# Layer 1 of the second half with W1 as weights, in a DLRM tower kernel

## The chip, the cores and the metric

The kernel runs on one core of one Trainium2 chip. The metric is the device time of one execution in microseconds (us).

## What is computed

Every one of 512 samples has 26 embedding rows of 128 numbers, looked up in 26 tables by `ids`, and one row of dense features. The dot products of all pairs of these 27 vectors and the dense row go through a tower of three layers:

```python
combined = concat([dense[:, None, :], e], axis=1)             # 512 x 27 x 128
pairs = einsum('bfd,bgd->bfg', combined, combined)[:, iu, ju]  # 351 pairs, i < j
h = concat([dense, pairs, dense], axis=1)                      # 512 x 607
h = maximum(h @ W_top1 + b_top1, 0.0)                          # 512 x 512
h = maximum(h @ W_top2 + b_top2, 0.0)                          # 512 x 256
y = h @ W_top3                                                 # 512 x 1
```

## The kernel before

All of it is written out by hand for five engines, with semaphores, and each engine runs its own list in order. Ten small tables are looked up as products with one-hot matrices (L415, L416, the first 50 us); the rows of the other sixteen tables are gathered by 64 indirect DMAs that GpSimd issues (L369), four to a group of 32 samples, and turned on TensorE by `turn_group` (L426) and, for the last group, in two halves by `turn_last` (L434). ScalarE copies each turned group into `eT`, where every sample has its vectors side by side.

`gram_chunk(n)` (L450) makes the dot products of 32 samples from `eT`: eight products in full float32, for which the trace shows 16 weight loads and 16 matmuls. Chunk 15 is made in two halves, the second one once the second half of the last group (group 16) is in `eT`. The two halves of `gram` hold chunks of even and odd number, and ScalarE and VectorE each copy half the rows of a chunk to `dots` (L680, L703). Four chunks are one tile of 128 samples. For each tile VectorE turns and repacks `dots` into `band` (`flip_tile`, L967 to L972; `flip_last_tile`, L988 to L996, where ScalarE takes a part), and TensorE turns `band` in three pieces so that the pairs lie on the partitions (`turn_pairs`, L459; `turn_last_pairs`, L467 and L472). ScalarE rounds the result to `pT_hi` (a type, float32r, whose products take one pass), and VectorE keeps the rest in `pT_lo`. In the same way all weights and activations are a high and a low part, and a product of two such operands is three matmuls: high by high, high by low, low by high.

**Layer 1 has two forms.** For the first half of the samples (tiles 0 and 1) W1 is the weight operand and the 256 samples of the half are the moving one, so its output has the units of layer 1 on the partitions, as layer 2 needs it. For tiles 2 and 3 it is the other way round (`rows_products`, L552): the 128 samples of a tile are the weights and 512 or 256 columns of W1 move past them. The output has samples on the partitions, so it is rectified into `h1_rows` (L834, L1013), turned by `turn_h1` (L595), rounded to `h1_hi` by `h1_rows_split` (ScalarE, L703) and the rest put in `h1_lo` by `h1_rows_rest` (VectorE, L1020). In tile 3 this goes in two banks, numbered 3 (units 256 to 511) and 4 (units 0 to 255).

Layer 2 of a tile starts with the bias, `layer2_bias` (L524, L525): two products of a single partition, a row of ones by the high and the low part of b2. Then come four steps of three products (`layer2_step`, L529 to L531). Layer 3 is one operation of VectorE for a tile (L1041).

PSUM tiles are used in turn: `look` has two banks in the order of `LOOK_ORDER`, and `look_bank` waits until the bank's use two places earlier has been read. `turn_pairs(2)` is two places behind layer 2 of tile 0, so it waits for `layer3(0)` on VectorE. `late` has two banks in the order of `LATE_ORDER`.

Of the kernel before, what the change touches and what calls it, by code (L numbers as in the profile page):

```python
# [24 lines left out]
P = 128  # L25
# [112 lines left out]
LOOK_ORDER += [("group", 14), ("group", 15), ("h1", 2), ("group", 16), ("turn", 3), ("layer2", 2), ("h1", 3), ("h1", 4)]  # L138
# [18 lines left out]
def late_on_act(what):  # L157
    return what[0] == "table" or what in (("rows", 2), ("rows", 4))
# [6 lines left out]
ROWS_OUT = 3 * 32 + NF  # L165


def build(nc, dense, ids_rows_first, ids_rows, ids_bcast, gathered, padded, w1, w2, b2, w3, out):
    with ExitStack() as ctx:
# [35 lines left out]
        b2_sb = sb("b2_sb", [1, H2])  # L205
        b2_hi = sb("b2_hi", [1, H2], F32R)
        b2_lo = sb("b2_lo", [1, H2], F32R)
        one_row = sb("one_row", [1, P], F32R)
# [3 lines left out]
        h1_rows = x_rows[:, :, :].rearrange("p t d -> p (t d)")  # L212
# [38 lines left out]
        w_sum = sem("w_sum")  # L251
        w_hi = sem("w_hi")
# [10 lines left out]
        pT_lo_ready = sem("pT_lo_ready")  # L263
        y_ready = sem("y_ready")
# [38 lines left out]
        def _(sp):  # L303
# [37 lines left out]
            sp.dma_start(b2_sb[:, :], b2).then_inc(w_in, 16)  # L341
            sp.dma_start(w3_sb[:, :], w3.to_broadcast([P, H2])).then_inc(w_in, 16)
            wait_look_done(sp, ("layer2", TILES - 2))
            sp.wait_ge(y_ready, 2)
# [30 lines left out]

        def late_layer2(t):

            q = 0 if t == TILES - 1 else CHUNK_Q // 2
            return gram[:, t // 2, q:q + H2 // P, :].rearrange("b q n -> b (q n)")

        @block.tensor
        def _(pe):
# [130 lines left out]
            def layer2_bank(t):  # L513
                if t in (0, 2):
                    return look[:, LOOK["layer2", t] % 2, 0:H2]
                return late_layer2(t)

            def layer2_bias(t):
                if t in (0, 2):
# [49 lines left out]
            def rows_3(n):  # L569
                return late[:, LATE["rows", n] % 2, 0:H1 // 2], slice(H1 // 2, H1) if n == 3 else slice(0, H1 // 2)  # L570
# [570 lines left out]
```

## Time and profile before

| what | us |
|---|---|
| median of 3 runs (112.5 to 112.81) | 112.67 |
| the profiled execution | 112.72 |
| its span, first to last instruction | 111.0 |
| TensorE busy in the span | 103.1 |
| VectorE, ScalarE, GpSimd busy | 79.7, 74.0, 71.9 |

The granted TensorE clock is 1.00 of full speed over the span. The 1.72 us between the profiled execution's time and its span lie before its first and after its last instruction. Names such as `late` and `look` in the rows are the PSUM tiles; the type "f32" of a matmul stands for float32 and for float32r. In the trace a matmul's length includes the time in which it drains, so lengths of neighbours overlap; the time that one takes from TensorE is read from start to start, or from the chain. In the chain, "x12" is twelve instructions of one line in a row.

### The profile page before, as it was taken

How to read it: one execution, taken by the hardware profiler on the slowest of the kernel's cores; microseconds unless marked ns; L12 is line 12 of the kernel's file. 1: busy time of each engine (PE TensorE's matmuls, PEld its weight loads, DVE VectorE, ACT ScalarE, POOL GpSimd, SP SyncE). 2: the span in 40 equal slices, each digit the busy share in tenths (PEclk: the TensorE clock that was granted, in tenths of full speed). 3: DMA queues.
4: the chain of work that ended last, by engine and by line, in shares of the span. 5: the costliest groups of instructions: out<-in, count | busy, mean ns of one | idle time of the engine just before them, and what ended most of it. 6: DMA issues, size and time to landing. Idle time of an engine off the chain costs nothing.

```text
span 111.0 us, 1932 instructions
## 1 busy us (share of the span) xinstructions
PE 103.1 (93%) x670; PEld 90.3 (81%) x670; DVE 79.7 (72%) x184; ACT 74.0 (67%) x131; POOL 71.9 (65%) x73
## 2 busy tenths in 40 slices
PE   3999999699999999989999989999999999999971
PEld 3965788577888888667999979999999998988760
DVE  5389999959999998972177996988348750596421
ACT  3347988999999999698578754759342563744030
POOL 6977778778877777777777777777777772000000
DMA  1899876892598279994211122112221111000000
GB/s 42 247 285 348 260 248 180 321 301 66 159 289 310 64 294 269 368 350 125 56 47 47 47 62 59 50 47 53 56 62 47 47 47 47 6 0 3 0 0 1
DMA packets 7195, 14.74 MB, mean 133 GB/s; under 512 B 1937, under 2 KB 2578, under 8 KB 7186
## 3 DMA queue, kind: packets, MB, share of 16 engines
q1 hardware_dynamic: 4850, 10.36, 27.9%
q0 software_dynamic: 2048, 4.20, 14.0%
q8 instruction: 5, 0.08, 0.4%
q10 hardware_dynamic: 288, 0.07, 0.3%
q14 instruction: 4, 0.03, 0.1%
HBM read 14.62 MB, written 0.00 MB: 132 GB/s over the span
## 4 chain that ended last, share of the span: by engine, by line
PE 50%; ACT 20%; DMA 13%; DVE 10%; issue 3%; SPq 1%; ACTq 0%; DVEq 0%
PE gram L450 25%; DMA table<-in_tbl 13%; ACT eT L703 7%; ACT table_hi L703 6%; DVE onehot L909 5%; PE late L552 5%; PE late L501 4%; DVE table_lo L903 3%; ACT distance L719 3%; PE look L426 3%; ACT onehot L723 2%; PE gram L529 1%; PE late L415 1%; PE look L529 1%; PE late L416 1%
## 5 line engine op out<-in xcount | busy, mean ns | idle before, releaser
L369 POOL DMA_INDIRECT e_rows<-in_gathered,idx x64 | 68.4, 1068 | 19.4 <-issue 19.4
L415 PE MATMUL late<-onehot,table_hi 128*128 128x512 f32 x84 | 34.3, 409 | 2.2 <-ACT eT L703 1.4
L416 PE MATMUL late<-onehot,table_lo 128*128 128x512 f32 x84 | 33.2, 395 | 0.0
L450 PE MATMUL gram<-eT 128*123 128x108 f32 x256 | 29.6, 271 | 0.6 <-ACT dots L703 0.3
L909 DVE TENSOR_SCALAR onehot<-ids,row_of_partition 128x512 fp32r<-128x512 int32 x69 | 29.8, 480 | 0.3 <-DMA ids<-in_ids_bcast 0.3
L450 PEld LDWEIGHTS gram<-eT 128*123 128x123 f32 x256 | 28.6, 187 | 1.0 <-ACT eT L703 0.5
L415 PEld LDWEIGHTS late<-onehot,table_hi 128*128 128x128 f32 x84 | 16.0, 190 | 8.0 <-ACT eT L703 2.3
L680 DVE COPY dots<-gram 32x216 f32<-32x216 f32 (+3 forms) x34 | 12.6, 371 | 11.2 <-PE gram L450 10.7
L703 ACT ACTIVATE dots<-gram 32x216 f32<-32x216 f32 (+1 forms) x34 | 11.2, 330 | 11.9 <-PE gram L450 11.7
L416 PEld LDWEIGHTS late<-onehot,table_lo 128*128 128x128 f32 x84 | 16.1, 191 | 3.0
L903 DVE TENSOR_TENSOR table_lo<-table,table_hi 128x384 fp32r<-128x384 f32 (+2 forms) x29 | 15.5, 536 | 2.7 <-ACT table_hi L703 2.7
L703 ACT ACTIVATE table_hi<-table 128x1024 fp32r<-128x1024 f32 (+2 forms) x11 | 11.1, 1013 | 5.3 <-DMA table<-in_tbl 5.3
L703 ACT ACTIVATE eT<-look 128x512 f32<-128x512 f32 (+1 forms) x18 | 11.6, 649 | 2.4 <-PE look L426 2.2
L703 ACT ACTIVATE eT<-late 128x512 f32<-128x512 f32 x10 | 11.0, 1097 | 0.4 <-PE late L416 0.4
L719 ACT ACTIVATE distance<-ids,row_of_partition 128x512 f32<-128x512 int32 x15 | 10.6, 706 | 0.0
L723 ACT ACTIVATE onehot<-distance 128x512 fp32r<-128x512 f32 x15 | 9.5, 633 | 1.3
L426 PE MATMUL look<-ident,e_rows 128*128 128x128 f32 x60 | 8.8, 272 | 0.0
L426 PEld LDWEIGHTS look<-ident,e_rows 128*128 128x128 f32 x60 | 7.1, 142 | 0.8
L618 PE MATMUL gram<-ident 128*128 128x128 f32 x18 | 4.2, 430 | 1.7 <-POOL ident L356 1.7
L618 PEld LDWEIGHTS gram<-ident 128*128 128x128 f32 x18 | 3.9, 331 | 1.7 <-POOL ident L356 1.7
L703 ACT ACTIVATE pT_hi<-look 126x384 fp32r<-126x384 f32 (+1 forms) x4 | 3.0, 754 | 1.6 <-PE look L467 1.5
L834 ACT ACTIVATE x_rows<-late 128x512 f32<-128x512 f32 (+1 forms) x2 | 1.0, 490 | 4.5 <-PE late L552 4.5
(103 smaller groups left out, 112.9 us busy)
## 6 DMA issues: line engine op xcount, KB each, us to landing
table<-in_tbl SPq DMA_DIRECT2D x7, 512.0 KB, 3.6
ids<-in_ids_bcast SPq DMA_DIRECT2D x10, 256.0 KB, 4.0
w_raw<-in_w SPq DMA_DIRECT2D x7, 256.0 KB
table<-in_tbl SPq DMA_DIRECT2D x2, 640.0 KB, 3.8
e_rows<-in_gathered,idx POOLq DMA_INDIRECT x64, 2.8
table<-in_tbl SPq DMA_DIRECT2D x2, 256.0 KB, 4.1
x_rows<-in_dense SPq DMA_DIRECT2D x1, 256.0 KB, 4.7
w_sb<-in_w SPq DMA_DIRECT2D x1, 128.0 KB
```

The costliest lines, as they stand in the source:

```text
L369: pool.indirect_dma_start(out=e_rows[:, c % GROUPS_AHEAD, k, :], out_offset=None, in_=gathered[:, :], in_offset=bass.IndirectOffsetOnAxis( ...
L415: pe.matmul(bank, table_hi[0:KP, i % 2, c, :], hot, start=c == 0, stop=False)
L416: last = pe.matmul(bank, table_lo[0:KP, i % 2, c, :], hot, start=False, stop=c == CHUNKS[i] - 1)
L426: last = pe.transpose(bank[:, k * P:(k + 1) * P], e_rows[:, c % GROUPS_AHEAD, k, :], ident[:, :])
L450: last = pe.matmul(gram[0:ROWS_OUT, n % 2, q, 0:QUADS * NG_COL], eT_flat[:, b * SLOTS:b * SLOTS + ROWS_OUT], eT[:, b:b + QUADS, 0:NG_COL], ...
L618: pe.matmul(gram[:, 0, 0, :], ident[:, :], ident[:, :], start=True, stop=True)
L680: return copy(dots[rows, t % 2, :, q0 + a:q0 + b], gram[rows, n % 2, a:b, j * NG_COL:(j + 1) * NG_COL].rearrange("f q g -> f g q"))
L703: return act.activation(dst, src, ACT.Copy)
L719: act.activation(distance[0:KP, n % 2, :], ids[0:KP, i % IDS_RING, :], ACT.Abs, bias=row0[CHUNKS[i]][0:KP, c:c + 1], scale=-1.0).then_inc( ...
L723: act.activation(onehot[0:KP, (free + OH_RING) % OH_RING, :], distance[0:KP, n % 2, :], ACT.Relu, bias=1.0, scale=-1.0).then_inc(onehot_ac ...
L903: dve.tensor_tensor(table_lo[0:KP, i % 2, a:c, :], table[0:KP, i % 2, a:c, :], table_hi[0:KP, i % 2, a:c, :].bitcast(F32), ALU.subtract).t ...
L909: dve.tensor_scalar(onehot[0:KP, n % OH_RING, :], ids[0:KP, i % IDS_RING, :], row0[CHUNKS[i]][0:KP, c:c + 1], None, ALU.is_equal).then_inc ...
```

## The change

- Layer 1 of tiles 2 and 3 is made one block of 128 units at a time, with W1 as weights and the tile's 128 samples as the moving operand. `rows_products` becomes `tile_products`: 12 products of 512 columns in tile 2 become 48 of 128 columns, and 24 products of 256 columns in tile 3 (6 for the dense row, 18 for the pairs) become 12 and 36 of 128 columns.
- The output has the units on the partitions. `turn_h1` and its eight transposes, the rectifying copies to `h1_rows` and three uses of `look` go. `h1_tile_split` (ScalarE) rectifies and rounds straight from `late`, and `h1_tile_rest` (VectorE) makes the low part.
- `layer2_bias` is one product of all 128 partitions: `bias_rows` has ones in rows 0 and 32 and zeros elsewhere, `b2_rows` the high part of b2 in row 0 and the low part in row 32. VectorE fills both with four memsets before it waits for the weights, and b2 is loaded to 33 partitions instead of one.
- Layer 2 of tile 2 goes to the bank of group 16. Its steps 2 and 3 move from before the last layer 1 to behind it. The last tile's layer 2 takes the products with `h1_hi` first and those with `h1_lo` behind them.
- On VectorE the low part of tile 2 moves from between the two halves of chunk 15's copies to before chunk 14's; `layer3(2)` moves behind the low parts of tile 3. `layer3(2)` reports on `y_ready`, and the output's DMA waits for that alone.

```diff
-LOOK_ORDER += [("group", 14), ("group", 15), ("h1", 2), ("group", 16), ("turn", 3), ("layer2", 2), ("h1", 3), ("h1", 4)]
+LOOK_ORDER += [("group", 14), ("group", 15), ("group", 16), ("turn", 3)]
...
-        one_row = sb("one_row", [1, P], F32R)
+        b2_sb = sb("b2_sb", [LO_ROW + 1, H2])
+        b2_rows = sb("b2_rows", [P, H2], F32R)
+        bias_rows = sb("bias_rows", [P, P], F32R)
...
+        def tile_units(n):
+
+            return late[:, LATE["rows", n] % 2, 0:(4 if n == 2 else 2) * P].rearrange("u (k b) -> u k b", b=P)
+
+        def tile_h1(h1, n):
+
+            ks = {2: slice(0, N1), 3: slice(2, N1), 4: slice(0, 2)}[n]
+            t = min(n, TILES - 1)
+            return h1[:, ks, t % 2 * P:(t % 2 + 1) * P]
...
+            if t == 2:
+                return look[:, LOOK["group", NCK] % 2, 0:H2]
             q = 0 if t == TILES - 1 else CHUNK_Q // 2
             return gram[:, t // 2, q:q + H2 // P, :].rearrange("b q n -> b (q n)")
...
             def layer2_bias(t):
-                if t in (0, 2):
+                if t == 0:
                     look_bank(("layer2", t))
+                elif t == 2:
+                    wait_look_done(pe, ("group", NCK))
                 else:
                     pe.wait_ge(dots_act, NCK if t == 3 else NCK - 1)
                     pe.wait_ge(dots_dve, NCK if t == 3 else NCK - 1)
-                pe.matmul(layer2_bank(t), one_row[0:1, :], b2_hi[0:1, :], start=True, stop=False)
-                pe.matmul(layer2_bank(t), one_row[0:1, :], b2_lo[0:1, :], start=False, stop=False)
+                pe.matmul(layer2_bank(t), bias_rows[:, :], b2_rows[:, :], start=True, stop=False)
...
-            def rows_products(t, bank, weights, units, start=False, stop=False):
+            def tile_products(t, out, weights, unit, start=False):
...
+                units = slice(unit * P, (unit + 1) * P)
                 for side, w, k in weights:
                     if k == KT:
-                        left = (x_hi, x_lo)[side][:, cols]
-                        right = w[:, KT, units]
+                        last = pe.matmul(out, w[:, KT, units], (x_hi, x_lo)[side][:, cols], start=start, stop=False,
+                                         skip_group_check=True)
                     else:
-                        left = (pT_hi, pT_lo)[side][0:KR, k, pair_cols]
-                        right = w[0:KR, k, units]
-                    last = pe.matmul(bank, left, right, start=start, stop=stop)
+                        last = pe.matmul(out, w[0:KR, k, units], (pT_hi, pT_lo)[side][0:KR, k, pair_cols],
+                                         start=start, stop=False, skip_group_check=True)
                     start = False
                 return last
...
             def layer1_rows_2():
-                bank = late_bank(("rows", 2))
-                units = slice(0, H1)
-                rows_products(2, bank, DENSE, units, start=True)
+                late_bank(("rows", 2))
+                out = tile_units(2)
+                for n in range(N1):
+                    tile_products(2, out[:, n, :], DENSE, n, start=n == 0)
...
-                for k in range(KT):
-                    rows_products(2, bank, [(0, w1_hi, k), (0, w1_lo, k)], units)
+                for n in range(N1):
+                    tile_products(2, out[:, n, :], [(0, w, k) for k in range(KT) for w in (w1_hi, w1_lo)], n)
                 wait_look_done(pe, ("turn", 2))
-                rows_products(2, bank, [(1, w1_hi, k) for k in range(KT - 1)], units)
-                rows_products(2, bank, [(1, w1_hi, KT - 1)], units, stop=True).then_inc(late_full, 1)
...
+                for n in range(N1):
+                    last = tile_products(2, out[:, n, :], [(1, w1_hi, k) for k in range(KT)], n)
+                last.then_inc(late_full, 1)
+
+            LAST_UNITS = [(3, 0, 2), (3, 1, 3), (4, 0, 0), (4, 1, 1)]
 
             def layer1_rows_3_dense():
-                for n in (3, 4):
-                    late_bank(("rows", n))
-                    bank, units = rows_3(n)
-                    rows_products(3, bank, DENSE, units, start=True)
+                for bank, j, n in LAST_UNITS:
+                    if j == 0:
+                        late_bank(("rows", bank))
+                    tile_products(3, tile_units(bank)[:, j, :], DENSE, n, start=j == 0)
...
             def layer1_rows_3():
                 for k in range(KT):
                     pe.wait_ge(pT_hi_ready, 3 + k + 1)
-                    for n in (3, 4):
-                        bank, units = rows_3(n)
-                        rows_products(3, bank, [(0, w1_hi, k), (0, w1_lo, k)], units)
+                    for bank, j, n in LAST_UNITS:
+                        tile_products(3, tile_units(bank)[:, j, :], [(0, w1_hi, k), (0, w1_lo, k)], n)
                 wait_look_done(pe, ("turn", 3))
                 pe.wait_ge(pT_lo_ready, KT - 1)
-                for n in (3, 4):
-                    bank, units = rows_3(n)
-                    rows_products(3, bank, [(1, w1_hi, k) for k in range(KT - 1)], units)
-                    rows_products(3, bank, [(1, w1_hi, KT - 1)], units, stop=True).then_inc(late_full, 1)
-
-            def turn_h1(n, ks):
-                bank = look_bank(("h1", n))
-                wait_late_done(pe, ("rows", n))
-                for k in ks:
-                    last = pe.transpose(bank[:, k * P:(k + 1) * P], h1_rows[:, k * P:(k + 1) * P], ident[:, :])
-                last.then_inc(look_full, 1)
+                for bank, j, n in LAST_UNITS:
+                    last = tile_products(3, tile_units(bank)[:, j, :], [(1, w1_hi, k) for k in range(KT)], n)
+                    if j:
+                        last.then_inc(late_full, 1)
 
...
             def layer2_rows_3():
-                wait_look_done(pe, ("h1", 3))
-                for k in (2, 3):
-                    layer2_step(3, k, False)
-                wait_look_done(pe, ("h1", 4))
-                for k in (0, 1):
-                    last = layer2_step(3, k, k == 1)
+                t = TILES - 1
+                rows = slice(t % 2 * P, (t % 2 + 1) * P)
+                for n, ks in ((3, (2, 3)), (4, (0, 1))):
+                    pe.wait_ge(h1_hi_ready, n + 1)
+                    for k in ks:
+                        pe.matmul(layer2_bank(t), h1_hi[:, k, rows], w2_hi[:, k, :], start=False, stop=False)
+                        pe.matmul(layer2_bank(t), h1_hi[:, k, rows], w2_lo[:, k, :], start=False, stop=False)
+                    wait_late_done(pe, ("rows", n))
+                    for k in ks:
+                        last = pe.matmul(layer2_bank(t), h1_lo[:, k, rows], w2_hi[:, k, :], start=False,
+                                         stop=n == 4 and k == ks[-1])
                 last.then_inc(last_full, 1)
...
             layer1_rows_2()
             turn_last(0)
             gram_chunk(14)
-            turn_h1(2, range(N1))
             turn_last(1)
             gram_chunk(15, range(CHUNK_Q // 2))
             gram_chunk(15, range(CHUNK_Q // 2, CHUNK_Q))
             layer1_rows_3_dense()
             layer2_first_half(1)
-            layer2_rows_2((0, 1))
+            layer2_rows_2((0,))
             turn_last_pairs(0)
-            layer2_rows_2((2,))
+            layer2_rows_2((1,))
             turn_last_pairs(1)
             turn_last_pairs(2)
-            layer2_rows_2((3,))
             layer2_bias(3)
             layer1_rows_3()
-            turn_h1(3, (2, 3))
-            turn_h1(4, (0, 1))
+            layer2_rows_2((2, 3))
             layer2_rows_3()
...
+            def h1_tile_split(n):
+                if n == 2:
                     wait_look_full(act, ("layer2", 0))
                 else:
                     act.wait_ge(last_full, 1)
-                wait_look_full(act, ("h1", n))
-                copy(h1_hi[:, ks, t % 2 * P:(t % 2 + 1) * P],
-                     look[:, LOOK["h1", n] % 2, :].rearrange("n (k b) -> n k b", k=N1)[:, ks, :]).then_inc(h1_hi_ready, 1)
+                wait_late_full(act, ("rows", n))
+                act.activation(tile_h1(h1_hi, n), tile_units(n), ACT.Relu).then_inc(h1_hi_ready, 1)
...
-            copy(one_row[:, :], one_col[0:1, :])
-            copy(b2_hi[:, :], b2_sb[:, :]).then_inc(w_hi, 1)
+            act.wait_ge(bias_zero, 4)
+            copy(b2_rows[0:LO_ROW + 1, :], b2_sb[:, :]).then_inc(w_hi, 1)
...
-            relu_rows(2, slice(0, H1))
+            h1_tile_split(2)
             last_group(0)
             dots_chunk(14)
             last_group(1)
-            h1_rows_split(2, slice(0, N1))
             last_dots()
             flat_half()
             first_band_block()
             turn_hi(3)
-            relu_rows(4, slice(0, H1 // 2))
-            h1_rows_split(3, slice(2, N1))
-            h1_rows_split(4, slice(0, 2))
+            h1_tile_split(3)
+            h1_tile_split(4)
...
+            dve.memset(b2_rows[:, :].bitcast(F32), 0.0).then_inc(bias_zero, 1)
+            dve.memset(bias_rows[:, :].bitcast(F32), 0.0).then_inc(bias_zero, 1)
+            dve.wait_ge(bias_zero, 2)
+            dve.memset(bias_rows[0:1, :].bitcast(F32), 1.0).then_inc(bias_zero, 1)
+            dve.memset(bias_rows[LO_ROW:LO_ROW + 1, :].bitcast(F32), 1.0).then_inc(bias_zero, 1)
...
+            def h1_tile_rest(n):
                 dve.wait_ge(h1_hi_ready, n + 1)
-                dve.tensor_tensor(h1_lo[:, ks, cols],
-                                  look[:, LOOK["h1", n] % 2, :].rearrange("n (k b) -> n k b", k=N1)[:, ks, :],
-                                  h1_hi[:, ks, cols].bitcast(F32), ALU.subtract).then_inc(look_dve, 1)
+                dve.scalar_tensor_tensor(out=tile_h1(h1_lo, n), in0=tile_units(n), scalar=0.0,
+                                         in1=tile_h1(h1_hi, n).bitcast(F32),
+                                         op0=ALU.max, op1=ALU.subtract).then_inc(late_dve, 1)
...
+            h1_tile_rest(2)
             dots_chunk(14)
             last_dots(0)
-            h1_rows_rest(2, slice(0, N1))
             last_dots(1)
             flip_last_tile()
             layer3(1)
             turn_lo(3)
+            h1_tile_rest(3)
+            h1_tile_rest(4)
             layer3(2)
-            relu_rows_3()
-            h1_rows_rest(3, slice(2, N1))
-            h1_rows_rest(4, slice(0, 2))
             layer3(3)
```

## Rows read from the trace of the kernel before

**Rows 1.** The page, part 1: busy time by engine.

```profile
PE 103.1 (93%) x670; PEld 90.3 (81%) x670; DVE 79.7 (72%) x184; ACT 74.0 (67%) x131; POOL 71.9 (65%) x73
```

**Rows 2.** Windows: busy time and count of each engine in two stretches of the end.

```profile
core 0: us, PE busy (x) PEld busy (x) DVE busy (x) ACT busy (x) POOL busy (x), PEclk, DMA share, GB/s
98.00:103.00 5.00, 5.00 (x35) 4.33 (x36) 3.81 (x13) 1.85 (x5) 0.00 (x0) 1.00 0.00 2
103.00:106.90 3.90, 2.89 (x23) 2.38 (x22) 1.39 (x6) 1.07 (x3) 0.00 (x0) 1.00 0.00 0
```

**Rows 3.** Chain that ended last, 90 to 98 us: start, length, what.

```profile
90.19 2.79 PE late L552 x12
...
93.20 1.71 PE gram L450 x16
94.91 0.44 PE look L595 x4
...
97.27 0.72 PE late L552 x6
```

**Rows 4.** The same chain where layer 2 of tile 2 begins.

```profile
100.03 0.31 PE look L524
100.34 0.12 PE look L525
100.46 0.31 PE look L529
100.77 0.12 PE look L530
```

**Rows 5.** The same chain from the last layer 1 to the end.

```profile
102.84 1.99 PE late L552 x15
...
104.93 0.44 DVE x_rows L1013
...
105.50 0.42 PE look L595 x2
...
106.90 0.38 PE gram L529
...
108.47 0.13 PE gram L531
```

**Rows 6.** Timeline of TensorE and its weight loads: start, length, engine, line, instruction.

```profile
97.01 0.19 PEld L552 LDWEIGHTS late<-w_hi,x_hi 128*128 128x128 f32 x1
97.12 0.19 PEld L552 LDWEIGHTS late<-table_lo,x_hi 128*128 128x128 f32 x1
...
97.04 0.36 PE L552 MATMUL late<-w_hi,x_hi 128*128 128x256 f32 x1
97.24 0.28 PE L552 MATMUL late<-table_lo,x_hi 128*128 128x256 f32 x1
```

**Rows 7.** Timeline of VectorE and the weight loads, 84 to 88 us.

```profile
84.49 1.08 DVE L967 STREAM_TRANSPOSE flip<-dots 128x864 f32<-128x864 f32 x1
...
87.25 0.14 DVE L1041 DVE_READ_ACCUMULATOR look<-look,w_sb 128x1 f32 x1
...
87.45 0.36 PEld L459 LDWEIGHTS look<-ident,band 128*126 128x126 f32 x3
```

**Rows 8.** Timeline of TensorE and ScalarE around gram chunk 14's end.

```profile
94.74 0.60 PE L595 MATMUL look<-ident,x_rows 128*128 128x128 f32 x4
95.18 0.38 PE L434 MATMUL look<-ident,e_rows 128*128 128x128 f32 x2
...
94.94 0.69 ACT L703 ACTIVATE dots<-gram 32x216 f32<-32x216 f32 x2 [1.03 <-PE gram L450]
95.66 0.40 ACT L703 ACTIVATE eT<-look 128x256 f32<-128x256 f32 x1
```

**Rows 9.** Timeline of VectorE and ScalarE, the last tile's pairs.

```profile
100.14 0.40 DVE L996 COPY band<-flat 128x238 f32<-128x238 f32 x1
...
99.71 0.32 ACT L703 ACTIVATE band<-flat 128x126 f32<-128x126 f32 x1
```

More of the change, by code:

```diff
@@ L157, in late_on_act @@
 def late_on_act(what):
-    return what[0] == "table" or what in (("rows", 2), ("rows", 4))
+    return what[0] == "table"
 LATE_ACT = [w for w in LATE_ORDER if late_on_act(w)]
@@ L165 @@
 ROWS_OUT = 3 * 32 + NF
+LO_ROW = 32
 def build(nc, dense, ids_rows_first, ids_rows, ids_bcast, gathered, padded, w1, w2, b2, w3, out):
@@ L251, in build @@
         w_sum = sem("w_sum")
+        bias_zero = sem("bias_zero")
         w_hi = sem("w_hi")
@@ L263, in build @@
         pT_lo_ready = sem("pT_lo_ready")
+        third_full = sem("third_full")
         y_ready = sem("y_ready")
@@ L600, in layer2_rows_2 @@
                     layer2_bias(2)
-                    wait_look_done(pe, ("h1", 2))
+                    wait_late_done(pe, ("rows", 2))
                 for k in ks:
@@ L604, in layer2_rows_2 @@
                 if ks[-1] == N1 - 1:
-                    last.then_inc(look_full, 1)
+                    last.then_inc(third_full, 1)
             def layer2_rows_3():
-                wait_look_done(pe, ("h1", 3))
-                for k in (2, 3):
-                    layer2_step(3, k, False)
-                wait_look_done(pe, ("h1", 4))
-                for k in (0, 1):
-                    last = layer2_step(3, k, k == 1)
+                t = TILES - 1
[9 more added lines that the diff above has]
+                                         stop=n == 4 and k == ks[-1])
                 last.then_inc(last_full, 1)
@@ L828, in h1_split @@
                         "n (k b) -> n k b", k=2), ACT.Relu).then_inc(h1_hi_ready, 1)
-            def relu_rows(n, units):
-                if n > 2:
-                    wait_look_full(act, ("h1", 2))
-                wait_late_full(act, ("rows", n))
-                act.activation(h1_rows[:, units], late[:, LATE["rows", n] % 2, 0:units.stop - units.start],
-                               ACT.Relu).then_inc(late_act, 1)
-            def h1_rows_split(n, ks):
-                t = min(n, TILES - 1)
-                if t == 2:
+            def h1_tile_split(n):
+                if n == 2:
                     wait_look_full(act, ("layer2", 0))
@@ L1008, in turn_lo @@
                                           ).then_inc(pT_lo_ready if k else look_dve, 1)
-            def relu_rows_3():
-                wait_look_full(dve, ("h1", 2))
-                wait_late_full(dve, ("rows", 3))
-                dve.tensor_scalar(h1_rows[:, H1 // 2:], late[:, LATE["rows", 3] % 2, 0:H1 // 2], 0.0, None, ALU.max
-                                  ).then_inc(late_dve, 1)
-            def h1_rows_rest(n, ks):
-                t = min(n, TILES - 1)
-                cols = slice(t % 2 * P, (t % 2 + 1) * P)
+            def h1_tile_rest(n):
                 dve.wait_ge(h1_hi_ready, n + 1)
-                dve.tensor_tensor(h1_lo[:, ks, cols],
-                                  look[:, LOOK["h1", n] % 2, :].rearrange("n (k b) -> n k b", k=N1)[:, ks, :],
-                                  h1_hi[:, ks, cols].bitcast(F32), ALU.subtract).then_inc(look_dve, 1)
+                dve.scalar_tensor_tensor(out=tile_h1(h1_lo, n), in0=tile_units(n), scalar=0.0,
+                                         in1=tile_h1(h1_hi, n).bitcast(F32),
+                                         op0=ALU.max, op1=ALU.subtract).then_inc(late_dve, 1)
             def h1_rest(h):
@@ L1034, in layer3 @@
             def layer3(t):
-                if t in (0, 2):
+                if t == 0:
                     wait_look_full(dve, ("layer2", t))
@@ L1038, in layer3 @@
                 else:
-                    dve.wait_ge(last_full, 1 + t // 2)
+                    if t == 2:
+                        dve.wait_ge(third_full, 1)
+                    else:
+                        dve.wait_ge(last_full, 1 + t // 2)
                     bank = late_layer2(t)
@@ L1042, in layer3 @@
                                                 op0=ALU.max, op1=ALU.mult, accum_out=y[:, t:t + 1])
-                done.then_inc(look_dve if t in (0, 2) else y_ready, 1)
+                done.then_inc(y_ready if t else look_dve, 1)
             dots_chunk(0)
@@ L1067, in _ @@
             dve.wait_ge(w_hi, K1 + N1 + 1)
-            dve.tensor_tensor(b2_lo[:, :], b2_sb[:, :], b2_hi[:, :].bitcast(F32), ALU.subtract).then_inc(w_lo, 1)
+            lo_row = slice(LO_ROW, LO_ROW + 1)
+            dve.tensor_tensor(b2_rows[lo_row, :], b2_sb[lo_row, :], b2_rows[lo_row, :].bitcast(F32), ALU.subtract
+                              ).then_inc(w_lo, 1)
             h1_rest(0)
```

13 lines of the change are left out of this document (3 added, 10 removed).

## Prediction

> **What bounds the kernel now.** I read the page's busy times first, then the windows of the end, then the chain, then the timelines where the chain changes engine. TensorE is busy 103.1 of 111.0 us, far ahead of VectorE with 79.7 [rows 1]. In the windows the reader should see two regimes. From 98 to 103 us TensorE has no free time. From 103 to 106.9 it is busy 2.89 of 3.90 us, because layer 1's last output waits to be turned and rounded [rows 2]. So TensorE work taken away or added before about 105 us counts in full unless a wait stands behind it. After that, latency between engines counts.
>
> **Pitches.** A matmul with weights of its own takes from start to start: 2.79/12 = 0.2325 us with 512 moving columns; 0.72/6 = 0.12 with 256, or closer, from 107.28 to 108.47 in ten steps behind the first product of the last layer 2, 0.118; 1.71/16 = 0.107 for the gram's 123 weight and 108 moving columns; 0.44/4 = 0.110 for a transpose of 128 by 128 [rows 3, 5]. From 256 to 512 columns the pitch doubles, from 256 to about 110 it hardly falls. A float32r weight load shows the floor: two follow each other by 0.11 us (97.01, 97.12), and the matmul that starts with its load is 0.36 us long where the next is 0.28 [rows 6]. The changed layer 1 has 128 moving float32r columns, which no row shows. The bounds are 0.059 us (half of 0.118, if only moving columns counted) and 0.2325 (the 512-column price, if short float32r products ran at a quarter of the rate). I take 0.109, between the gram and the transposes, which are nearest in both shapes.
>
> **Tile 2's layer 1.** 48 x 0.109 = 5.23 for 2.79 [rows 3]: +2.44. It stands between two blocks of a full TensorE.
>
> **The turn of tile 2.** Its four transposes, 0.44, go [rows 3], but they cover a wait. Without them `turn_last(1)` starts at 94.74 instead of 95.18, the first half of chunk 15 at 94.96, and the second half wants its weights after eight more instructions (0.86) less the 0.11 by which a load runs ahead, at 95.7. That half needs group 16 in `eT`. ScalarE copies chunk 14's dots from 94.94 and then group 16 from 95.66 for 0.40, so until 96.06 [rows 8], and neither moves relative to chunk 14. The stall is 0.36 plus about 0.04 for the release. The transposes' 0.44 becomes a wait of 0.40: -0.04.
>
> **Tile 3's layer 1.** Dense part: 12 x 0.109 = 1.31 for 0.72 [rows 3], +0.59. Pairs: 36 x 0.109 = 3.92 for 18 x 0.118 = 2.12, +1.80.
>
> **The bias.** The chain spends 0.31 on the first one-partition product, 0.12 on the second and 0.31 on the first full product behind them; the next full one takes 0.12 [rows 4]. So a step from full height to one partition or back costs 0.19 beyond the pitch. One product of full height leaves 0.12 + 0.12 of 0.74: -0.50 per tile, four tiles. For tiles 1, 2 and 3 TensorE is full and all of it counts: -1.50. For tile 0, at about 84 us, it does not. Behind its layer 2 and a gram chunk comes `turn_pairs(2)`, which waits until `layer3(0)` has read the bank. VectorE begins to repack tile 2's pairs at 84.49, driven by chunk 11 and not by layer 2, and ends `layer3(0)` at 87.39; the weight load of `turn_pairs(2)` starts at 87.45 [rows 7]. With 0.50 less work TensorE arrives at 86.95 and waits 0.50: nothing gained. If the cover were absent, this would be worth -0.50.
>
> **The end.** Now 15 of layer 1's 18 products are done at 104.83, so the last at 104.83 + 3 x 0.118 = 105.18, and the last product of layer 2 at 108.60 [rows 5]. Of these 3.42 us twelve products take 1.42. The other 2.00 are latency: rectifying (VectorE, 0.44), four transposes, rounding and low part, one behind the other.
> After the change bank 3 is complete six products (0.65) before the end E of layer 1. ScalarE's rectifying and rounding is one operation of 256 columns, 0.40 [rows 8], the low part on VectorE another, 0.44 [rows 5]. With 0.2 for draining and release, the high part of bank 3 is there at E, its low part at E+0.45, those of bank 4 at E+0.6 and E+1.05. TensorE runs layer 2 of tile 2, steps 2 and 3, until E+0.71 and asks for these four at E+0.71, E+1.18, E+1.4 and E+1.9. None is late. So -2.0, and the two moved steps cost the same 0.71 in their new place.
> Do the moved steps leave a hole where they stood? They covered the last tile's pairs. Let T be the end of chunk 15 (97.1 now). `band` is ready on ScalarE at 100.03 (T+2.9) and on VectorE at 100.54 (T+3.4) [rows 9]. With the low part of tile 2 out of VectorE's way they can only come earlier, and TensorE has the dense part, 1.31, layer 2 of tile 1, 13 x 0.118 = 1.53, and bias and a step, 0.47: and asks for them at T+3.3 and T+3.8: no wait either way. The rounding of the first piece (0.3 for the transpose, 0.4 on ScalarE) lands within 0.05 of when it is wanted.
>
> **At nothing.** The four memsets stand where VectorE next waits for the weight loads, before the first gram chunk's copies. b2's load to 33 partitions is queued on SyncE ahead of w3's to 128, and both are waited for together, as before. ScalarE and VectorE each handle one narrow operation as before. If this cover were gone it would be a few tenths. The output DMA waits for one semaphore instead of two; `layer3(2)`, now behind the low parts, ends over 0.5 us before `layer3(3)` can begin. VectorE's early low part of tile 2 waits for ScalarE's; queued behind it are only chunk 14's dots, a gram chunk (1.71) later.
>
> **Sum.** 2.44 - 0.04 + 0.59 + 1.80 - 1.50 - 2.0 = +1.3 us. The profiled execution took 112.72, its span 111.0 and 1.72 around it, which I leave alone. It is 0.05 above the median of 112.67. So 114.0.
>
> **Rivals.**
> *A, the forecast* (0.57): weight loads set the pitch, 0.107 to 0.111. With the smaller or larger of them the sum moves by 0.2.
> *B, the two hidden waits are not there* (0.11). If ScalarE's copy of group 16 and `layer3(0)` are not what TensorE meets, 0.40 and 0.50 come back: 113.1. Against it stand the times of [rows 7, 8]; for it, that a wait inferred to within 0.1 us can shrink.
> *C, faster: short products are cheap* (0.10). If a float32r load can hide beneath a matmul faster than 0.11, all 96 products gain. The point at which the change breaks even is 0.109 - 1.3/96 = 0.095 us. At 0.059 the 96 products take 4.8 less: 109.2, or some tenths more since the pairs' repacking would then be waited for. For it: no row has a stream of float32r loads bound by nothing else. Against it: the loads of [rows 6], and a gram that gains nothing from having only 108 columns.
> The Trainium skill (TensorE: Matmul & The Clock Gate, Back-to-back issue gap) puts a sustained stream of load and matmul pairs at about 81 ns for 128 columns. By that figure the sum would be 96 x 0.028 = 2.7 us lower, an estimate of 111.3; the trace's own pairs, at 107 to 110 ns, do not agree with it.
> *D, short float32r products are dear* (0.10). At full float32's two passes, 2 x 0.107, the 96 cost 10.1 more: 124. At 0.2325 they cost 11.9 more, 126. The kernel before has no float32r product under 256 columns, so nothing excludes this.
> *E, the pitch of 256 columns is a floor for float32r* (0.12): 96 x 0.009 = 0.9 more, 114.9. For it: it is the nearest price within the type.
>
> **How the numbers follow.** The likeliest case gives 114.0. The range takes A, B and E with 0.2 of slack: 112.9 to 115.1, leaving out C and D. About 0.3%, 0.34 us, is what a measurement of this kernel can tell from no change. Faster is C, 0.10. Within 0.3% are the lower edge of B and a C near its break-even point, 0.07. The rest is slower, 0.83.
>
> **What would show it.** Right: 48 matmuls of `tile_products` in tile 2 in about 5.2 us; a TensorE hole of 0.5 before `turn_pairs(2)` and of 0.4 in the middle of chunk 15; 0.12 for a bias product and for its follower; 36 products in 3.9; layer 2 of tiles 2 and 3 at the end as 18 products without a gap, 2.1 us. Wrong: a pitch of the 128-column products under 0.095 turns the sign; one over 0.13 leaves the range above; a gap ahead of the last tile's layer 2 means that ScalarE or VectorE is later than worked out; a clock under 1.00 would make every term of TensorE too small.

## The result, and the profile of the changed kernel

The changed kernel takes 114.81 us (median of four runs, 114.71 to 115.31) where the kernel before took 112.74 beside it: a ratio of 1.0175, interval 1.0107 to 1.0243. Six more runs on another chip gave 115.27 against 112.82 for the kernel before, 1.0245 (1.0203 to 1.0287). The ratios, here and below, are those of the record; they are not the quotients of the medians and can differ from these by up to 0.004. The forecast was 114.0 us with a range of 112.9 to 115.1. The direction was right, and the first median lies in the range; the second one, 115.27, lies 0.2 above its upper end. Of a rise of 2.1 us (2.45 on the other chip) the forecast had 1.3.

The profiled execution took 114.71 us with a span of 112.9. The page, part 1, of the changed kernel:

```profile
PE 105.6 (94%) x718; PEld 95.1 (84%) x718; DVE 80.3 (71%) x187; ACT 73.2 (65%) x128; POOL 72.4 (64%) x73
```

TensorE has 48 matmuls more than in [rows 1] and 2.5 us more work, in a kernel that it bounds. The chain that ended last, in the changed kernel, from `layer3(0)` to the last tile's dense part (start, length, what):

```profile
87.34 0.50 DVE look L1040 x2
...
87.89 0.55 PE look L473 x3
...
90.57 1.29 PE late L563 x12
91.86 4.02 PE late L566 x36
...
98.59 0.41 ACT eT L713
...
99.04 1.11 PE gram L464 x8
100.15 1.31 PE late L563 x12
```

L563 and L566 are the products of `tile_products`: 48 in 5.32 us, 0.111 each, where [rows 3] had 12 in 2.79. The two entries of VectorE and ScalarE are waits that the kernel before did not have. The weight loads show them, with the releaser at the end of the line:

```profile
87.88 0.31 PEld L473 LDWEIGHTS look<-ident,band 128*126 128x126 f32 x3 [0.39 <-DVE look L1040]
...
99.04 0.93 PEld L464 LDWEIGHTS gram<-eT 128*123 128x123 f32 x8 [0.32 <-ACT eT L713]
```

The first is `turn_pairs(2)` behind `layer3(0)`, the second the second half of chunk 15 behind the copy of group 16. The same chain at the bias of tiles 1 and 2 and at the end:

```profile
101.46 0.17 PE gram L540
101.62 0.12 PE gram L544
...
103.03 0.12 PE look L540
103.15 0.12 PE look L544
...
104.32 4.03 PE late L566 x36
108.35 0.17 PE look L544
...
110.29 0.25 PE gram L625 x2
```

The bias is one product of 0.12 to 0.17, and its follower 0.12, where [rows 4] had 0.31, 0.12 and 0.31. Behind layer 1 (36 products in 4.03, 0.112 each) come 18 products in 2.18 us without a gap, where [rows 5] had 3.42 for twelve.

**Where the rest is.** Two stretches have to be told apart. From the first gram product to the end of the span it is 111.0 - 52.93 = 58.1 us before and 112.9 - 53.37 = 59.5 after. The spans are given to 0.1 us only. The start of the last `layer3` is given to 0.01, and nothing but the output's transfer comes behind it. Before and changed:

```profile
52.93 5.41 PE L450 MATMUL gram<-eT 128*123 128x108 f32 x48 [0.27 <-ACT eT L703]
...
108.62 0.43 DVE gram L1041
```

```profile
53.37 5.41 PE L464 MATMUL gram<-eT 128*123 128x108 f32 x48 [0.27 <-ACT eT L713]
...
110.56 0.43 DVE gram L1040
```

In each pair the first line is from the timeline and the second from the chain. That is 55.69 us before and 57.19 after: +1.50, all in places that the change touches. Ahead of the first gram product lies the table stage. No instruction of it was changed, and yet it is 0.44 longer in this profile. The table gives both stretches for every kernel that follows; "first table" is when ScalarE starts to copy the first one-hot table's result to `eT`, "to layer 3" is from the first gram product to the start of the last `layer3`.

| kernel | median, us | ratio to before | first table | first gram product | from there to layer 3 | from there to the end |
|---|---|---|---|---|---|---|
| before | 112.67 | | 14.09 | 52.93 | 55.69 | 58.1 |
| changed | 114.81 | 1.0175 (1.0107-1.0243) | 14.75 | 53.37 | 57.19 | 59.5 |
| c_after, changed again | 115.27 | 1.0245 (1.0203-1.0287) | 14.52 | 53.79 | 57.19 | 59.5 |
| e1_before_new_bias | 111.47 | 0.9894 (0.9869-0.9918) | 14.08 | 52.88 | 54.23 | 56.6 |
| e2_after_old_bias | 116.51 | 1.0347 (1.0310-1.0383) | 14.68 | 53.71 | 58.68 | 61.0 |
| e6_tile2_old_form | 111.74 | 0.9921 (0.9893-0.9948) | 13.85 | 52.36 | 54.74 | 57.0 |
| e3_gram13_first | 114.64 | 1.0157 (1.0114-1.0199) | 14.66 | 54.20 | 56.80 | 59.1 |
| e4_steps_ahead | 115.12 | 1.0208 (1.0162-1.0255) | 14.77 | 53.81 | 57.22 | 59.5 |
| e5_dense_in_chunk15 | 114.51 | 1.0162 (1.0118-1.0205) | 14.43 | 53.34 | 56.88 | 59.2 |
| e7_bias_and_order | 111.00 | 0.9819 (0.9770-0.9867) | 14.00 | 53.59 | 53.55 | 55.9 |
| e8_before_spare | 116.87 | 1.0358 (1.0315-1.0402) | 14.84 | 54.01 | 55.72 | 61.3 |
| e9_after_fewer | 114.00 | 1.0102 (1.0051-1.0152) | 13.99 | 52.82 | 57.10 | 59.4 |
| e10_bias_gram_first | 111.22 | 0.9861 (0.9817-0.9905) | 14.05 | 53.60 | 53.92 | 56.3 |

The median of before is that of its first three runs; beside the experiments it took 112.82 (c_after, e1, e2, e6), 112.64 (e3, e4, e5, e7) and 112.78 us (e8, e9, e10). The last four columns are from one profiled execution each. The stretch to layer 3 repeats where its code is the same: 57.19 twice for the changed kernel, and 55.69 and 55.72 for before and e8. So it resolves what the medians, whose runs scatter by half a microsecond and more, cannot.

### The profile page after: what moved, and what is told of

It is laid out like the page before. It is cut to its first block, busy times and chain, and to the rows that moved or that the text cites. A ratio compares the mean times of both kernels' runs of the same rounds, so it can differ in the third digit from the quotient of the medians.

```text
span 112.9 us, 2022 instructions
## 1 busy us (share of the span) xinstructions
PE 105.6 (94%) x718; PEld 95.1 (84%) x718; DVE 80.3 (71%) x187; ACT 73.2 (65%) x128; POOL 72.4 (64%) x73
## 4 chain that ended last, share of the span: by engine, by line
PE 68%; ACT 10%; DMA 10%; DVE 6%; issue 2%; SPq 1%; DVEq 0%; ACTq 0%
PE gram L464 23%; PE late L429 11%; PE late L430 11%; DMA table<-in_tbl 10%; PE late L566 7%; ACT eT L713 4%; PE look L440 4%; PE late L515 4%; ACT table_hi L713 3%; PE late L563 2%; DVE onehot L908 1%; ACT dots L713 1%; DVE table_lo L902 1%; ACT distance L729 1%; DVE flip L971 1%
## 5 line engine op out<-in xcount | busy, mean ns | idle before, releaser
L430 PE MATMUL late<-onehot,table_lo 128*128 128x512 f32 x84 | 33.8, 402 | 0.0
L1016 DVE SCALAR_TENSOR_TENSOR onehot<-late,onehot 128x256 fp32r<-128x256 f32 (+1 forms) x3 | 1.5, 514 | 8.7 <-ACT onehot L846 8.7
L846 ACT ACTIVATE onehot<-late 128x256 fp32r<-128x256 f32 (+1 forms) x3 | 1.4, 456 | 7.8 <-PE late L566 7.8
L566 PE MATMUL late<-pT_hi,w_hi 126*128 126x128 f32 x24 | 5.5, 275 | 0.0
```

The costliest lines, as they stand in the source:

```text
L430: last = pe.matmul(bank, table_lo[0:KP, i % 2, c, :], hot, start=False, stop=c == CHUNKS[i] - 1)
L566: last = pe.matmul(out, w[0:KR, k, units], (pT_hi, pT_lo)[side][0:KR, k, pair_cols], start=start, stop=False, skip_group_check=True)
```

## The experiments

### The changed kernel again: c_after

> The changed kernel again, for comparison on the same chip. It was 2.07 us slower by the medians of four runs. In its profile 0.44 us of this is there already when layer 1 of the first half starts (69.73 against 69.29 us), before any product that the change touches. Theory 1: this is a difference between executions in the table stage, so in this profile the start of layer 1's first dense product lies elsewhere again, and the true cost is about 1.5 us (1.3%). Theory 2: b2's load to 33 partitions or the memsets cause it; it is there again, 0.3 to 0.5 us late, and the cost stays at 2.0 us.

In the chain the first dense product of layer 1 starts at 70.15 (69.29 before, 69.73 in the first profile), again late. So the cost behind the table stage is 1.50 us a second time, and the late table stage is no accident of one execution. By the medians the cost is 2.45 us, above what either theory said. Theory 1 falls on the early part. Whether theory 2's cause is right, the next two tell.

### The bias alone: e1_before_new_bias and e2_after_old_bias

```diff
-                pe.matmul(layer2_bank(t), one_row[0:1, :], b2_hi[0:1, :], start=True, stop=False)
-                pe.matmul(layer2_bank(t), one_row[0:1, :], b2_lo[0:1, :], start=False, stop=False)
+                pe.matmul(layer2_bank(t), bias_rows[:, :], b2_rows[:, :], start=True, stop=False)
```

with b2's load, the memsets and the splits that belong to it. e1 puts this into the kernel before, e2 takes it out of the changed one.

> The kernel before, with the bias as one product of full height and nothing else of the change. Theory 1 (a switch to one partition and back costs 0.19 us each way, hidden for tile 0): the two products and the late first step shrink from 0.74 to 0.24 us per tile; tile 0's gain turns into a wait before turn_pairs(2), tiles 1 to 3 count: 1.5 us faster than before. Theory 2 (b2's wider load and the memsets delay the early stage by 0.4): 1.1 us faster. A third: if the 0.31 in the chain is the first product's own start and not the switch, only the second product is saved, 0.12 per tile: 0.4 us faster.

> The changed kernel with the old bias of two one-partition products, the old load of b2 and no memsets. Theory 1: 1.5 us slower than the changed kernel, 3.0 to 3.5 slower than before, and the wait before turn_pairs(2) is gone. Theory 2 (the early 0.44 belongs to b2's load or the memsets): only 1.1 slower than the changed kernel, and the first dense product of layer 1 starts 0.4 earlier than there.

From the first gram product to layer 3, e1 is 1.46 us shorter than before (by the medians 112.82 - 111.47 = 1.35) and e2 1.49 longer than the changed kernel (116.51 - 115.27 = 1.24, which by itself lies nearer to theory 2's 1.1): three tiles at just under 0.5, in both surroundings. In e2 the chain shows the old price at tile 0, and no wait behind it:

```profile
84.33 0.31 PE look L540
84.64 0.12 PE look L541
84.76 0.31 PE look L545
85.08 0.12 PE look L546
...
88.52 0.33 PE look L473 x3
```

`turn_pairs(2)` takes 0.33 there, against 0.55 with its wait in the changed kernel. As for theory 2: e1 has the wider load and the memsets, and its first table is done at 14.08, as before; e2 has neither, and its first table comes at 14.68, as in the changed kernel; its first dense product starts at 70.08 in the chain, not 0.4 earlier. b2's load and the memsets are not what delays the table stage.

### Tile 2 in the old form: e6_tile2_old_form

```diff
...
-                for n in range(N1):
-                    tile_products(2, out[:, n, :], DENSE, n, start=n == 0)
...
+                rows_products(2, bank, DENSE, units, start=True)
...
             gram_chunk(14)
+            turn_h1(2, range(N1))
             turn_last(1)
```

> The changed kernel with tile 2's layer 1 in the old form (12 products of 512 columns, then turned), tile 3 in the new one. Theory 1 (the pitch of 128-column products, 0.112 us in the profile, is the cost): 36 fewer products save 48 x 0.112 - 2.79 = 2.6 us, the transposes cost 0.44 and cover the 0.32 wait in chunk 15, the low part of tile 2 goes back into VectorE's chain, where nothing waits for it: 2.5 us faster than the changed kernel, 0.5 to 1.0 faster than before. Rival (the cost is the lost cover, not the products): under 1 us faster than the changed kernel.

To layer 3 it is 54.74, 2.45 under the changed kernel, as theory 1 said. By the medians it is 3.5 under c_after; the other 1.1 lies ahead of the first gram product, and so outside the edit. The chain:

```profile
89.60 2.79 PE late L583 x12
...
94.32 0.44 PE look L602 x4
...
94.97 1.71 PE gram L465 x16
```

The 16 instructions of chunk 15 take 1.71 again: the wait for group 16 is gone with the transposes back. The cost is in the products. By differences, tile 2's new form costs 2.45 us, the bias gives back 1.46, and what is left, 1.50 - 2.45 + 1.46 = +0.5, is tile 3's new form with everything at the end: more products for less latency, nearly even.

### The wait for `layer3(0)`: e3_gram13_first and e10_bias_gram_first

```diff
             gram_chunk(12)
-            turn_pairs(2)
             gram_chunk(13)
+            turn_pairs(2)
```

> The changed kernel with gram chunk 13 before turn_pairs(2) instead of behind it. Theory 1 (TensorE waits there for layer3(0), and the saved bias of tile 0 is lost in it): the wait of 0.4 us before turn_pairs(2) goes, everything behind starts 0.4 earlier, 0.4 us faster than the changed kernel. Rival (the next wait takes its place, because chunk 14's dots or group 14 come later): no change.

> The kernel before with the new bias and gram chunk 13 ahead of turn_pairs(2), nothing else. Theory 1 (tile 0's bias is lost in the wait for layer3(0)): the 0.4 to 0.5 us that e1 left is gained too; from the first gram product to the end 56.2 us instead of 56.62 in e1 and 58.07 before, the time 1.9 us under before. Rival (a later wait takes it): 56.6, as e1.

e3: 56.80 to layer 3, 0.39 less than the changed kernel. The weight loads run through where the wait was:

```profile
86.54 3.52 PEld L464 LDWEIGHTS gram<-eT 128*123 128x123 f32 x32
89.97 0.36 PEld L473 LDWEIGHTS look<-ident,band 128*126 128x126 f32 x3
```

e10: 53.92, 0.31 less than e1 (by the medians 1.56 under before, where 1.9 was expected). The bias of tile 0 was lost in that wait, and a change of order alone recovers most of it. Of the rest, 0.14 is a new wait: the twelve products of tile 2's layer 1 take 2.93 in e10's chain, 2.79 in [rows 3].

### The moved steps of layer 2: e4_steps_ahead

```diff
             turn_last_pairs(2)
+            layer2_rows_2((2, 3))
             layer2_bias(3)
             layer1_rows_3()
-            layer2_rows_2((2, 3))
```

> The changed kernel with steps 2 and 3 of tile 2's layer 2 put back ahead of the last layer 1, so that nothing stands between layer 1 and the last tile's layer 2. Theory 1 (the latency at the end is gone because of the form and the order of the products, not because of the moved steps): the high part of bank 3 is there 0.02 before layer 1's end in the profile and each later part just in time: at most 0.15 us slower. Rival (the moved steps are the cover): TensorE waits for the parts, 0.4 to 0.7 us slower.

57.22 to layer 3, 0.03 more than the changed kernel. TensorE goes from layer 1 straight into the last layer 2:

```profile
107.94 1.50 PE L566 MATMUL late<-pT_lo,w_hi 126*128 126x128 f32 x12
109.31 0.39 PE L621 MATMUL gram<-w_hi,onehot 128*128 128x256 f32 x1
109.53 0.28 PE L622 MATMUL gram<-onehot 128*128 128x256 f32 x1
```

The first product is long by 0.1. The moved steps hide nothing that was not hidden: what is left of the change at the end is enough. Of what is left (no transposes, bank 3 complete early, the products with `h1_hi` first) no run takes one part out alone.

### The wait in chunk 15: e5_dense_in_chunk15

```diff
             gram_chunk(15, range(CHUNK_Q // 2))
+            layer1_rows_3_dense(LAST_UNITS[:1])
             gram_chunk(15, range(CHUNK_Q // 2, CHUNK_Q))
-            layer1_rows_3_dense()
+            layer1_rows_3_dense(LAST_UNITS[1:])
```

> The changed kernel with three of the twelve dense products of tile 3 (0.33 us) between the halves of chunk 15. Theory 1 (the transposes of tile 2 had covered the copy of group 16): they fill the wait of 0.32 us, and the nine left still cover the last tile's pairs: 0.3 us faster than the changed kernel. Rival (the pairs are the limit at once, since chunk 15 ends as late as before): TensorE waits before turn_last_pairs instead, no change.

56.88 to layer 3, 0.31 less. Three dense products fill the hole, and the load of the second half waits no more:

```profile
98.86 0.19 PEld L563 LDWEIGHTS late<-x_lo,w_hi 128*128 128x128 f32 x1
99.04 0.94 PEld L464 LDWEIGHTS gram<-eT 128*123 128x123 f32 x8
```

### Why the table stage is late: e8_before_spare and e9_after_fewer

e8 adds to the kernel before, behind its last product:

```diff
             layer2_rows_3()
+            for _ in range(24):
+                pe.matmul(gram[:, 0, 0, :], ident[:, :], ident[:, :], start=True, stop=True)
```

e9 leaves out of the changed kernel the products with `table_lo` for the last five one-hot tables.

> The kernel before with 24 spare float32 products (48 loads and 48 matmuls in the trace, as many as the change adds) behind the last product of TensorE, into a bank that nobody reads any more. So far the six profiles of kernels with the new form in both tiles have the first table's result copied to eT at 14.43 to 14.77 us, the four others at 13.85 to 14.09. Theory 1 (the longer program of TensorE makes the first loads land later): 14.4 to 14.8 here. Theory 2 (it hangs on something else in those kernels): 13.8 to 14.1. In both the spare products take 48 x 0.107 = 5.1 us behind 108.6, so the span ends near 114 and the time is 2.5 to 3.5 us above before.

> The changed kernel without the products of the low parts of the last five one-hot tables (42 products fewer in the second half of the table stage; the output lacks these low parts). The first table is computed in full. Theory 1 (program length): the first table's result is copied at 13.8 to 14.1 us, as in the kernels with the old form. Theory 2: 14.4 to 14.8, as in the changed kernel. What happens behind the fifth table is not comparable; from the first gram product on it should be 59.5 us to the end, as in the changed kernel.

On ScalarE, the second table's rounding and the first table's copy. Before:

```profile
9.50 1.06 ACT L703 ACTIVATE table_hi<-table 128x1024 fp32r<-128x1024 f32 x1 [0.64 <-DMA table<-in_tbl]
...
14.09 1.11 ACT L703 ACTIVATE eT<-late 128x512 f32<-128x512 f32 x1
```

The kernel before with the spare products, which run 95 us later:

```profile
10.25 1.06 ACT L705 ACTIVATE table_hi<-table 128x1024 fp32r<-128x1024 f32 x1 [1.39 <-DMA table<-in_tbl]
...
14.84 1.12 ACT L705 ACTIVATE eT<-late 128x512 f32<-128x512 f32 x1
```

The changed kernel:

```profile
10.15 1.06 ACT L713 ACTIVATE table_hi<-table 128x1024 fp32r<-128x1024 f32 x1 [0.72 <-DMA table<-in_tbl]
...
14.75 1.13 ACT L713 ACTIVATE eT<-late 128x512 f32<-128x512 f32 x1
```

The changed kernel with 42 products fewer:

```profile
9.33 1.06 ACT L714 ACTIVATE table_hi<-table 128x1024 fp32r<-128x1024 f32 x1 [0.48 <-DMA table<-in_tbl]
...
13.99 1.11 ACT L714 ACTIVATE eT<-late 128x512 f32<-128x512 f32 x1
```

Adding matmuls that run at the very end delays the second table's load, and taking matmuls away, none of them of the first five tables, brings it back. SyncE issues this load at 2.65 us in every profile, so it is not issued later; it takes longer. In the chain it takes 6.83 us before, 7.57 in e8 and 7.48 in the changed kernel:

```profile
2.65 6.83 DMA table<-in_tbl
```

```profile
2.65 7.57 DMA table<-in_tbl
```

The pieces of the first table are not late: ScalarE rounds the first of them at 3.79 to 3.92 us in all thirteen profiles. Over all profiles the two groups do not touch: with 666 to 686 matmuls of TensorE the first table is copied at 13.85 to 14.09 (six profiles, mean 14.01), with 718 or 722 at 14.43 to 14.84 (seven, mean 14.66). The three chips that ran the experiments each had kernels of both groups. So the longer program costs about 0.65 us at the start. e8 adds instructions to TensorE alone, and e9 takes only some of TensorE's away; whether as many instructions of another engine would do the same, no run tells.

How much of it reaches the end? In e8 the first gram product is 1.08 late, in the two profiles of the changed kernel 0.44 and 0.86. This column scatters more: e7 and e10, with the shorter program, have 53.6. But the medians separate the groups as well. The median span of a kernel's runs, less its last column, is 52.8 to 53.3 us for the six shorter programs and 53.5 to 54.0 for the seven longer ones, 0.7 apart in the mean. e8's time shows the same: 2.5 to 3.5 us above before were expected, and it is 4.1 (116.87 against 112.78), 3.2 behind the first gram product and the rest ahead of it. In e9 only the first table and the stretch behind the gram can be compared. With less for TensorE to do, the granted clock was 0.87 between 40 and 53 us and 1.00 elsewhere.

Between 6 and 8 us the DMA engines are as busy in both but move less. The windows (busy time and count of TensorE, its weight loads, VectorE, ScalarE and GpSimd, then clock, DMA share and GB/s) of the kernel before and of e8:

```profile
6.00:8.00 2.00, 1.84 (x6) 1.54 (x7) 1.62 (x5) 1.05 (x2) 1.39 (x3) 1.00 0.98 292
```

```profile
6.00:8.00 2.00, 1.12 (x3) 0.96 (x4) 1.75 (x5) 1.05 (x2) 1.70 (x2) 1.00 0.99 166
```

e9 moves 283 GB/s there and the changed kernel 193; the six shorter programs move 258 to 299, the seven longer ones 159 to 193. That much is shown. Why is open. The profile counts one more packet of instruction loading in the longer programs (queue q8, 6 instead of 5), but in the changed kernel and in e8 it comes after 105 us, so it does not compete with the tables. No run separates the place of the program or of the tables in memory from its length.

### Both kernels beaten: e7_bias_and_order

The kernel before with the new bias, chunk 13 first, and this at the end:

```diff
-            layer2_rows_2((2,))
             turn_last_pairs(1)
             turn_last_pairs(2)
-            layer2_rows_2((3,))
             layer2_bias(3)
             layer1_rows_3()
+            layer2_rows_2((2,))
             turn_h1(3, (2, 3))
             turn_h1(4, (0, 1))
+            layer2_rows_2((3,))
             layer2_rows_3()
```

with the last transposes of `h1` in banks of the gram, and tile 2's layer 2 in the bank of group 16.

> The kernel before with the new bias, gram chunk 13 ahead of turn_pairs(2), and steps 2 and 3 of tile 2's layer 2 in the two gaps of the end (step 2 behind layer 1, step 3 behind the last transposes, which go to banks of the gram). Theory 1: 1.5 for the bias of tiles 1 to 3, 0.5 for that of tile 0, 0.7 for the moved steps, less some 0.1 where the last pairs are now waited for: 2.5 us faster than before, 110.2. Rival (the last tile's pairs become the limit as soon as TensorE has less to do in front of them): 1.5 to 2.0 faster.

Its ratio to before is 0.9819 (interval 0.9770 to 0.9867). By the medians it is 1.6 us faster (111.0 against 112.64), which is the rival's 1.5 to 2.0 and not the 2.5 expected. From the first gram product to layer 3 it is 2.1 us shorter, between the two. e10 has the same bias and the same order of chunk 13; beside it the moved steps, with the banks that they need, bring 0.4 of the 0.7 that was expected of them. A new wait, for VectorE's part of the last band, takes 0.2 of the rest, as the rival had it; the last layer 2 still waits for the low part, as before:

```profile
101.01 0.43 PE L484 MATMUL gram<-ident,band 128*126 128x128 f32 x2 [0.21 <-DVE band L1019]
```

```profile
105.42 0.19 PEld L542 LDWEIGHTS gram<-w_hi,onehot 128*128 128x128 f32 x1 [0.54 <-DVE onehot L1043]
```

## Why the prediction was right

The mechanism was right term by term behind the first gram product. That the first median lies in the range owes something to luck as well, since a cost of about 0.65 us was missing from the sum; the step that failed is named at the end of this section.

**The pitch.** The forecast took 0.109 for a product that no row showed, between the gram and the transposes. 96 products took 1.29 + 4.02 + 1.31 + 4.03 = 10.65 us, 0.111 each. The reason given is that the weight load sets the pitch. No run takes the load and the moving columns apart, but the rows favour it: the gram's products, with 123 weight and 108 moving columns, take 0.107, and 0.107/123 and 0.111/128 are the same 0.87 ns for a weight column, while for a moving column they are 0.99 and 0.87. Rivals C, D and E fall: neither 0.059 nor 0.214 nor 0.118. E named 114.9 us, the nearest to both medians, but that is chance, since its pitch is not the measured one. The figure of the Trainium skill (TensorE: Matmul & The Clock Gate, Back-to-back issue gap), 81 ns for 128 columns, does not hold for this type: the trace has 111 ns. The pitch made tile 2 cost 5.32 for 2.79, +2.53 instead of +2.44, and the pairs of tile 3 4.03 instead of 3.92.

**The two hidden waits.** 0.40 was forecast for group 16, 0.32 measured, and e5 fills it. 0.50 was forecast for `layer3(0)`, 0.39 measured, and e3 and e10 recover 0.3 to 0.4. Rival B falls: without these steps the sum would have been 0.9 lower.

**The bias.** -1.50 forecast, -1.46 and -1.49 measured. That the price lies in the step from full height to one partition and back, and not in the number of products, is what e1 shows: saving a product alone would have given 0.4. The Trainium skill (TensorEngine Tiling (Array Packing), Key Properties) says that a change of tiling mode drains TensorE. The 0.19 us each way would fit that, but no row here shows in which mode a product runs, so it is not shown that this is the cause.

**The end.** 2.0 of latency gone, forecast and measured: 3.42 us for 12 products became 2.18 for 18, and 2.18 - 0.71 is 1.47, so 1.95. The forecast allowed 0.2 for draining and release, for which it named no row; ScalarE starts on bank 3 at 107.77, 0.08 behind its last product. With E for the end of layer 1 (108.35), the four parts are ready at E-0.19, E+0.26, E+0.48 and E+0.93, each 0.1 to 0.2 earlier than forecast. That the moved steps cost nothing was right, and e4 adds that they bring nothing.

**The sum.** Behind the first gram product it says +1.3 and the profiles +1.50. The 0.002 us by which each of 96 products was dearer than 0.109 make 0.2 of it, the bias and the end together 0.1, and the shorter wait for group 16 takes 0.1 back.

**The step that failed** is the one called "at nothing". It put the early part of the kernel at no cost and looked for a cost only in b2's load and the memsets. e1 and e2 clear those. What costs 0.65 us there is that TensorE's program is 48 matmuls longer, in a stage where none of them runs, as e8 and e9 show. 1.50 + 0.65 = 2.15 us stands beside 2.07 and 2.45 for the differences of the medians. Why the length of the program has this effect stays open. Since nothing in the forecast allowed for it, the first median stayed inside the range only by the room left for a dearer pitch, and the second did not.

## What to carry to other kernels

In this kernel a float32r product with 128 weight and 128 moving columns takes 0.111 us, hardly less than the 0.118 of one with 256 moving columns. So cut a product into pieces of 128 moving columns only where the latency it saves, here 2.0 us once at the end, is worth 0.05 us more for every piece that replaces half of a 256-column product; in the middle of a full TensorE (tile 2) it is a plain loss. A product over one partition between full ones cost its own time and 0.19 us on either side here, and padding it to full height saved just under 0.5 us for a tile. When work is taken off the bound engine, look for the buffer it will reach early: two of the gains here turned into waits, and a change of order gave most of each back.

## What was not expected of the hardware

A program with 718 or 722 matmuls instead of at most 686 has the load of its second table land about 0.7 us later (rounded at 9.84 to 10.25 us against 9.20 to 9.50), though the load is issued at the same time and the instructions added in e8 run over 90 us afterwards. Among the programs of 666 to 686 matmuls the longest, e6, has the earliest first table, so it looks like a step rather than a slope; no run between 686 and 718 shows where it lies. The effect is large beside the changes measured here, and it sits outside the stage that was edited: comparing the stretch behind the edit and the stretch ahead of it separately is what made both visible.
